# Eight units of attention and experts on one core: per-row values by way of DRAM, and a new order of the steps

## What is computed

```
scores = x @ w + b                        # one score per row
top_scores, top_indices = top_k(scores, k = 204)       # in order of score
h  = x[top_indices] * sigmoid(top_scores)
z  = layernorm(h)
q, k, v = z@Wq.T+bq, z@Wk.T+bk, z@Wv.T+bv
P  = softmax(q k^T / 8)    (rows with q[0]==0 or k[0]==0 are zero)
h  = h + (P v) @ Wo.T + bo
xn = layernorm(layernorm(h)) * gamma + beta
logits = xn @ Wr + br                     # 8 experts
w  = softmax of the two largest logits
h  = h + sum over e of w[e] * (gelu(xn @ W1[e] + b1[e]) @ W2[e] + b2[e])
```

## Time and profile before

| | |
|---|---|
| three runs | 377.15, 377.46, 378.77 us, median 377.46 |
| the profiled execution | 378.94 us, its span 376.8 us |
| mean granted TensorE clock | 0.854 of 2.4 GHz |
| busy: PE, DVE, ACT, POOL | 296.2, 180.7, 148.7, 105.8 us |
| first phase, up to the first `hidden` | 0 to 229.6 us |
| expert steps | 229.6 to 369.4 us |

### The profile page before, as it was taken

The page is one execution under the profiler, slowest core; times in us unless marked ns, Lnnn a source line. Parts: engine busy times, 40 slices in busy tenths (PEclk is TensorE's granted clock), DMA queues, the critical chain, the costliest instruction groups (busy, mean ns, idle before and its releaser), DMA issues.

```text
span 376.8 us, 5432 instructions
## 1 busy us (share of the span) xinstructions
PE 296.2 (79%) x1883; PEld 167.3 (44%) x1883; DVE 180.7 (48%) x541; ACT 148.7 (39%) x328; POOL 105.8 (28%) x97
## 2 busy tenths in 40 slices
PE   1459759598787989888676747979797979797992
PEld 0338546467565666766464442323232323232230
DVE  3764755839458465631316213353544354444331
ACT  1112334333444344353533215444453535354551
POOL 3220200304022030303010110645453544354553
PEclk9975858888696969698886856999998999899997
DMA  2540000000000000000000007808081808170800
GB/s 51 152 121 2 0 0 3 0 3 0 2 0 2 0 3 0 2 0 2 2 0 0 3 20 164 178 5 179 25 191 34 180 12 190 36 168 26 179 22 23
DMA packets 13326, 18.64 MB, mean 49 GB/s; under 512 B 3756, under 2 KB 12276, under 8 KB 12276
## 3 DMA queue, kind: packets, MB, share of 16 engines
q1 hardware_dynamic: 12724, 18.17, 21.5%
q10 hardware_dynamic: 576, 0.13, 0.2%
HBM read 16.42 MB, written 1.88 MB: 49 GB/s over the span
## 4 chain that ended last, share of the span: by engine, by line
PE 61%; DVE 17%; issue 8%; ACT 7%; SPq 3%; POOL 2%; DMA 1%; POOLq 0%; ACTq 0%
PE PD L761 14%; PE PD L771 13%; PE PD L562 5%; DVE pick L843 4%; ACT E L419 4%; PE PD L644 4%; PE PD L614 4%; PE PD L633 3%; DVE nmax L872 3%; PE PD L593 2%; PE PD L550 2%; PE PD L601 2%; PE PD L689 2%; PE PD L661 2%; DVE ye L1026 2%
## 5 line engine op out<-in xcount | busy, mean ns | idle before, releaser
L499 ACT ACTIVATE hid<-PD,b_eff 128x816 f32<-128x816 f32 x64 | 60.1, 940 | 56.0 <-PE PD L761 56.0
L1026 DVE SCALAR_TENSOR_TENSOR ye<-PD,b_col,mb 128x408 f32<-128x408 f32 x64 | 41.0, 642 | 78.6 <-PE PD L771 73.1
L348 POOL TENSOR_TENSOR acc<-acc,ye 128x408 f32<-128x408 f32 x56 | 58.8, 1049 | 60.4 <-DVE ye L1026 59.6
L761 PE MATMUL PD<-uT,w_g 64*128 64x408 f32 x256 | 63.9, 579 | 0.0
L771 PE MATMUL PD<-hid,w_sb 128*64 128x408 f32 x256 | 59.7, 545 | 0.2 <-ACT hid L499 0.2
L327 POOL TENSOR_TENSOR rstd<-veps,neg_half 102x8 f32<-102x8 f32 x8 | 13.1, 1638 | 124.9 <-DVE veps L903 124.9
L419 ACT ACTIVATE E<-PD,nmax 102x204 f32<-102x204 f32 x64 | 26.7, 430 | 35.6 <-DVE nmax L872 35.6
L833 DVE SCALAR_TENSOR_TENSOR ahead<-PD,score,tie 128x256 bf16<-128x256 f32 x64 | 27.1, 479 | 22.4 <-PE PD L550 22.4
L761 PEld LDWEIGHTS PD<-uT,w_g 64*128 64x128 f32 x256 | 20.3, 193 | 31.9 <-issue 29.5
L633 PE MATMUL PD<-ident,E 102*102 102x102 f32 x128 | 18.1, 297 | 19.1 <-ACT rbc L401 13.6
L771 PEld LDWEIGHTS PD<-hid,w_sb 128*64 128x64 f32 x256 | 12.9, 138 | 39.5 <-issue 37.4
(11 more groups left out here) (130 smaller groups left out, 381.5 us busy)
## 6 DMA issues: line engine op xcount, KB each, us to landing
mb<-mixd SPq DMA_DIRECT2D x16, 816.0 KB, 8.0
X<-in_x SPq DMA_DIRECT2D x8, 256.0 KB, 4.9
out<-y SPq DMA_DIRECT2D x8, 204.0 KB
w_raw<-in_L_ffn_W SPq DMA_DIRECT2D x2, 256.0 KB, 3.3
w_sb<-in_L_ffn_W SPq DMA_DIRECT2D x1, 256.0 KB, 3.7
mixd<-mT SPq DMA_DIRECT2D x8, 25.5 KB, 1.5
w_bc<-in_L_tok_w ACTq DMA_DIRECT2D x1, 32.0 KB, 3.8
wq_nat<-in_L_attn_Wq ACTq DMA_DIRECT2D x1, 32.0 KB
```

The source lines that it names most:

```text
L348: pool.tensor_tensor(acc[n % 2][:, :], H[:, n, :] if e == 0 else acc[n % 2][:, :], ye[k % 4][:, :], ALU.add)\
L499: act.activation(hid[k % 2][:, :, :], hid_ps[k % 2][:, :, 0:C], ACT.Gelu, bias=b1_eff[:, e:e + 1]).then_inc(hid_ok, 1)
L761: last = pe.matmul(hid_ps[k % 2][:, p, 0:C], w1_g[halves[p], e, :], uT[halves[p], n, :], start=True, stop=True)
L1026: dve.scalar_tensor_tensor(out=ye[k % 4][:, :], in0=y_ps[k % 2], scalar=b2_col[:, e:e + 1], in1=mb[n % 2][:, e, :], op0=ALU.add, op1=ALU.m ...
```

## The change

1. The score rows, the first inverse deviations, the reciprocals of the softmax sums and the second inverse deviations are no longer spread by PE and copied by ACT. SP writes them to DRAM (`scored`, `rstdd`, `rdend`, `rstd2d`) and reads them back onto all partitions, from one in-order list of 10 DMAs and a load of X per step.
2. `tie` is one table of 257 columns and lies in PSUM, as does `row_no`; `one_hot` is in two halves. `scale_out` on POOL multiplies the attention's output, after a copy of it by ACT (`copy_OT`).
3. `project` is 8 matmuls of 64 x 64 weights and 204 columns in place of two of 128 x 128 and 408 columns, and q and k of the second pair stand on the other half of the partitions.
4. A unit now has lags 0 to 4, and the work of one step is in another order on every engine. The loop has 9 steps.
5. After it comes an end written out by hand, in which the last unit's attention alternates with the first expert steps. PE waits for the first unit alone (`u_ok` = 1). Routing of units 0, 1 and 2 is in steps 7, 8 and the end; that of unit n + 2 within expert steps 0 to 6 of unit n. There are three `mb` tiles.

```diff
-        A_STEPS = UNITS + A_LAG                     # 13
+        A_STEPS = UNITS + 1                         # 9
...
+            def write_scores(u):
+                sp.wait_ge(sc_ok, 2 * u + 2)
+                sp.dma_start(scored[u].rearrange("(b p t) -> p b t", b=UB, t=T),
+                             score[u % 2][:, :].rearrange("p (b t) -> p b t", t=T)).then_inc(scored_ok, 16)
+            def read_scores(u):
+                sp.wait_ge(scored_ok, 16 * (u + 1))
...
+                sp.dma_start(srow[u % 2]..., scored[u].partition_broadcast(P)).then_inc(srow_in[u % 2], 16)
+            def spread(dst, line, done):
+                for i, p in enumerate(halves):
+                    sp.dma_start(dst[p, :].rearrange("p (g q) -> p g q", q=Q),
+                                 line.rearrange("(g p) q -> p g q", p=2)[i].partition_broadcast(D)).then_inc(done, 16)
+            def write_std(u):
+                sp.wait_ge(rstd_ok, u + 1)
+                sp.dma_start(by_row(rstdd[u]), rstd[:, :], allow_slow_non_contiguous=True).then_inc(rstdd_ok, 16)
+            def read_std(u):
+                sp.wait_ge(rstdd_ok, 16 * (u + 1))
...
+                spread(rbc, rstdd[u], rb_in)
...
+            for s in range(A_STEPS):              # SP; unit(...) tests cut
+                load_x(s + 3)
+                write_std2(s - 3); write_den(s - 2); write_std(s); write_scores(s + 2)
+                read_std2(s - 3); read_den(s - 2); read_std(s); read_scores(s + 2)
+                if s >= UNITS - 1:
+                    write_mix(s - (UNITS - 1))
+                    read_mix(s - (UNITS - 1))
...
+            def scale_out(u):                     # POOL
+                pool.wait_ge(OT_ok, u + 1)
+                pool.wait_ge(rd_in, 32 * (u + 1))
...
+                pool.tensor_tensor(attn[:, :], OT[:, :], rdbc[:, :], ALU.mult).then_inc(attn_ok, 1)
...
+            for s in range(A_STEPS):              # ACT; unit(...) tests cut
+                softmax(s - 2, 0); copy_hT(s); squares2(s - 3); squares(s)
+                softmax(s - 2, 1); copy_ET(s - 2, 0); exp_neg(s + 2); copy_ET(s - 2, 1)
+                copy_q(s - 1); copy_k(s - 1); copy_OT(s - 2)
+                if s >= UNITS - 1:
+                    gap_tanh(s - (UNITS - 1))
+                    copy_mT(s - (UNITS - 1))
...
             def project(u):
                 pe.wait_ge(z_ok, u + 1)
                 if u >= 1:
-                    pe.wait_ge(ET_ok, 2 * u - 1)
-                pe.matmul(q_ps, wq_bd[:, :], zT[u % 2][:, :], start=True, stop=True).then_inc(qp_ok, 1)
-                pe.matmul(k_ps, wk_bd[:, :], zT[u % 2][:, :], start=True, stop=True).then_inc(kp_ok, 1)
+                    pe.wait_ge(ET_ok, 2 * u)
+                for i, w in enumerate((wq_bd, wk_bd)):
+                    for pr in range(2):
+                        for p in range(2):
+                            last = pe.matmul(qk_ps[halves[p ^ pr], pr, i * S:(i + 1) * S], w[halves[p], halves[p]],
+                                             zT[u % 2][halves[p], cols(pr, 0, R)], start=True, stop=True)
...
             def centre2(u):
                 pe.wait_ge(h1_ok, u + 1)
                 if u >= 1:
                     pe.wait_ge(u_ok, u)
...
             def hidden(k):
                 n, e = divmod(k, NE)
+                if k == 0:
+                    pe.wait_ge(act_prep, 4)
+                    pe.wait_ge(exp_ok, 2 * UNITS)
+                if k == 1:
+                    pe.wait_ge(ET_ok, 2 * UNITS)
...
+                if k % NE == 0:
+                    pe.wait_ge(u_ok, n + 1)
...
-            pe.wait_ge(u_ok, UNITS)
...
             def compare(u, pr):
-                dve.wait_ge(srow_ok, 2 * u + pr + 1)
+                dve.wait_ge(srow_in[u % 2], 16 * (u // 2 + 1))
...
-                    dve.scalar_tensor_tensor(out=ahead[:, i, :], in0=srow[:, b * N:(b + 1) * N], ...
-                                             in1=tie[:, t, :], ...
+                    dve.scalar_tensor_tensor(out=ahead[:, g, :], in0=srow[u % 2][:, b, :], ...
+                                             in1=tie_ps[:, 1 - t:1 - t + N], ...
...
-                    last = dve.tensor_scalar(pick[:, g, :], row_no[:, :], ...
+                    last = dve.tensor_scalar(pick[:, g, :], row_ps, ...
...
+            for s in range(A_STEPS):              # DVE; unit(...) tests cut
+                residual(s - 3); normalise2(s - 4); normalise(s - 1); row_max(s - 2, 1)
+                var_eps2(s - 3); compare(s + 1, 0); var_eps(s); one_over_den(s - 2); compare(s + 1, 1)
+                copy_v(s - 1); score_sum(s + 2); one_hot(s + 1, 0); gate_value(s + 2); one_hot(s + 1, 1)
+                row_max(s - 1, 0)                 # from step 7 on: route(s - 7, 0..3) among these, part 3 last
...
+            for k in range(8, K):
+                n, e = divmod(k, NE)
+                weighted(k)
+                if n + 2 < UNITS and e in (0, 1, 2, 4):
+                    route(n + 2, (0, 1, 2, 2, 3)[e])
```

More of the change, by code:

```diff
@@ L52, in audio_tower_kernel @@
     G = 4
+    MB = 3
     VX = D + 2
@@ L780, in turn_back @@
                 last.then_inc(backp_ok, 1)
[L782 to L795 removed]
+            pe.wait_ge(pool_prep, 3)
@@ new lines, in _ @@
+            centre2(UNITS - 2)
+            scores(UNITS - 1, 1)
+            logits(2)
+            variance2(UNITS - 2)
+            turn_exp(UNITS - 1, 0)
+            hidden(0)
+            turn_exp(UNITS - 1, 1)
+            attend(UNITS - 1, 0)
+            turn_mix(2)
+            hidden(1)
+            second(0)
+            attend(UNITS - 1, 1)
+            for k in range(2, 5):
+                hidden(k)
+                second(k - 1)
+            centre2(UNITS - 1)
+            hidden(5)
@@ L796, in _ @@
+            second(4)
+            variance2(UNITS - 1)
+            for k in range(6, K):
+                n, e = divmod(k, NE)
+                hidden(k)
+                second(k - 1)
+                if n >= 1 and e == 2:
+                    turn_back(n - 1)
+                if n >= 1 and n + 2 < UNITS:
+                    if e == 0:
                         logits(n + 2)
+                    if e == 6:
+                        turn_mix(n + 2)
+            second(K - 1)
             turn_back(UNITS - 1)
@@ new lines, in _ @@
+                if (u := unit(s, 1)) is not None:
+                    row_max(u, 0)
+                if s == UNITS - 2:
+                    dve.wait_ge(pick_ok, 2 * UNITS)
+                    dve.tensor_copy(fall_s, falling[:, :]).then_inc(dve_prep, 1)
+                    dve.wait_ge(dve_prep, 9)
+                if s >= UNITS - 1:
+                    route(s - (UNITS - 1), 3)
+            residual(UNITS - 2)
+            normalise2(UNITS - 3)
+            row_max(UNITS - 1, 1)
+            for part in range(3):
+                route(2, part)
```

656 lines of the change are left out of this document (326 added, 330 removed).

## The result

The changed kernel takes 463.3 us (median of 4 runs, 461.2 to 463.9) beside 378.0 for the kernel before: a ratio of 1.225, 95% interval 1.220 to 1.230. I had forecast 320, in a range of 302 to 352. The profiled execution has a span of 461.8 us.

| | predicted, us | measured, us |
|---|---|---|
| end of the first `row_max` | 53 | 65.8 |
| from there to `hidden(0)` | 127.2 | 239.9 |
| `hidden(0)` to `hidden(9)` | 25.3 | 33.9 |
| `hidden(9)` to the end of the span | 113.6 | 122.2 |

What follows compares the result with a forecast made beforehand. A ring of hand-overs bounds the first phase, no engine being full; PE bounds the experts. Head 53 + steps 121 + end and ramp 31.5 + experts 103.3 + rest 10.3 = 319.1 us span, forecast 320, range 302 to 352.

Steps and rivals of the forecast that it cites:

- L: Landing of one element-wise line write of 816 4-byte packets: taken as 3.5 us, from bounds of 1.9 to 6.7.
- The DMAs, the unknown: Section on each step's DMAs: issuing ten costs SP 5.5 us; a second ring through them takes 15.5 to 17.5 us.
- rival (a): The DMA ring sets the step, L of 6 to 8: 20.5 us per step, 337 us, up to 350; chance 0.22.
- the ring: Each step's second ring, from `residual` through the 1/den write and reads to `scale_out`: 12 to 14 us + L.
- rival (d): Slower than before: a step's three element-wise writes queue on few engines; 394 us at 28.6 us a step; chance 0.05.
- the first ring: Each step from `row_max` through `score_sum`, `exp_neg`, `copy_ET`, `project` and `scores`: 15.7 to 18.9 us by clock, taken as 18.
- The head: Start to the end of the first `row_max`: 53 us instead of 43, with scores going through DRAM before a comparison.
- The experts: From `hidden(9)` to `hidden(63)`: 103.3 us instead of 120.2, with `mix` made ahead and PE no longer standing still.
- The ramp: From `hidden(0)` to `hidden(9)`: 25.3 us, including 3 us of `turn_back(0)` waiting for `normalise2(7)`.
- the wait of `exp_neg`: On ACT in each step: `exp_neg` waits for `score_sum` ahead of the second `copy_ET`; PE idle some 3 us before `project`.
- the quadrants: `project` on PE as eight matmuls of 204 columns: 0.9 to 1.6 us, with no row to price it.

Runs made afterwards that it cites:

- runs 7, 8 and 10: run 1 plus one unread write of 816 4-byte pieces per unit, neighbours 4, 512 and 64 bytes apart: 387.6, 348.8 and 340.8 us.
- run 7: run 1 plus one write per unit of 816 4-byte pieces, neighbours 4 bytes apart, ahead of the write of 1/den: 387.6 us.
- run 2: The changed kernel with each of the three line writes issued as two DMAs, of 96 and 6 rows: 472.4 us, ratio 1.249.
- run 1: The changed kernel with its three line writes in 102 pieces of 32 bytes, values coming back in another order: 344.2 us, ratio 0.908.
- run 3: The changed kernel with only the write of 1/den in 4-byte pieces, those of 1/std and 1/std2 in 32-byte pieces: 379.4 us.
- run 6: run 5 with SP issuing the write and read of unit 0's scores earlier in its list: 316.0 us, ratio 0.831.
- run 4: The changed kernel with 1/std, 1/den and 1/std2 spread by PE and copied by ACT, without the line DMAs: 335.6 us, ratio 0.887.
- run 5: run 4 with `exp_neg` moved behind `copy_k` on ACT and `gate_value` behind `row_max` on DVE: 322.3 us, ratio 0.849.

## Why the prediction was wrong

**The step that failed is the landing of the element-wise writes, L**, in "The DMAs, the unknown". I took 3.5 us from bounds of 1.9 to 6.7. Measured: 13.2 to 15.0 us in a full step, 7.9 with one such write left, and even the very first, with no other line write near it (issued at 40.01, its read at 46.57), up to 6.6. The upper bound did not hold, and neither row had the pattern: the loads of 4-byte columns read neighbours from DRAM and wrote to separate partitions, the large packets were large. The trace of before had no row of many small pieces written close together into DRAM, and that is what costs (runs 7, 8 and 10). It is also no price per packet: in run 7 the records of these packets are nearly as short as my 7.7 ns, 9 ns, and the landing is late all the same. I had also counted L for one write, though three are issued within 2 us of each other; the sentence "one late write holds all" stood in rival (a), not in the sum.

By the Trainium skill (DMA: Bandwidth & Descriptors, section "Why a DMA increments its semaphore by 16 and not by 1") the write would go to 6 engines. No run here shows to how many it went; run 2 shows that dividing it otherwise does not shorten the landing, so the rule did not decide the time. That the rule gave 15.4 us at 102 ns a packet, beside a measured 15.0, is chance.

**The rule for the ring was right.** "It costs 1 us per step for each us of L over 4.5": L of 15 gives 10.5 us more than 18, a step of 28.5. The measured 34.1 has 5.6 more. Of these 4.0 are the reads (7.1 us from issue to `scale_out` instead of the 3.1 in the ring; in run 1, without the 4-byte pieces, 4.2 to 6.0 in the two steps compared below). The other 1.6 are computing, 12.0 us where I had at most 10.4. It runs at the lower clock (granted 0.50), for which I had allowed; but DVE stands 1.85 us for `variance2` and 0.89 for `variance` in it, and the ring as I listed it has neither.

**What happened is the ring of rival (a) with the queue of rival (d).** `residual` waits for a DMA in every step, the sign of (a), and the writes land after more than 10 us, the sign of (d). (a) stopped at L = 8 and 350 us. (d) had the three writes queue behind each other (run 3) and gave 394 us at a step of 28.6, but by a price per packet on few engines: its own formula, with the mean of 115 ns and 16 engines, gives 17.6 us, not 34. I gave (d) 0.05, since I let the 7.7 ns of a load stand against it.

**The clock came on top.** I had let the clock into the first ring (18 us for 15.7), but priced a longer L at 1 us for each us. In the changed kernel the granted clock is 0.65 in such steps; PE, idle for 13.6 us before 165.29, then takes 1.70 us for `centre2`, against 0.92 in run 6. In run 7 the wait for 1/den is 3.2 us longer than in run 1 (8.1 against 4.9), the step 6 (26.7 against 20.6). Of the rest, 0.3 us are the read's, and 2.6 the computing from `scale_out` to the next write, 12.3 us against 9.7. The two stretches, run 7 and run 1, with the granted clock as the third number from the end:

```profile
134.30:146.50 12.20, 9.88 (x41) 7.42 (x42) 5.33 (x18) 3.52 (x11) 3.39 (x3) 0.50 0.11 37
```

```profile
119.70:129.40 9.70, 7.34 (x47) 5.01 (x44) 4.95 (x18) 4.49 (x16) 3.13 (x3) 0.82 0.18 65
```

**The head was 12.8 us too short.** The scores came 4 us late: the first read was issued at 18.47 and the first comparison started at 25.09, not 21. Since `select` now starts on half of the picks, this cost only 1.6 us there (28.65 instead of 27). The picks read PSUM now, four in 1.68 us, 0.40 apart, not 0.31: 1.4 us for 16 picks. I had carried over the 23.7 us of the old order from the first `select` to the first `scores`; it is 34.1 here (28.65 to 62.70). Order is the larger part of that: `normalise(0)` belongs to the next step, on DVE behind the picks of unit 1 (to 47.0). Then it waits another 6.25 us for the fetched 1/std, so that `zT` starts at 53.27. Run 4, which has the same order and spreads by PE, takes 30.1 (28.11 to 58.20): 4.0 of the 10.4 us are the fetch.

**The experts were right.** They run with no wait for `mix`:

```profile
375.76 0.34 PE L749 MATMUL PD<-ident,mix 102*16 102x102 f32 x2
376.03 0.95 PE L765 MATMUL PD<-uT,w_g 64*128 64x408 f32 x4
376.92 0.91 PE L779 MATMUL PD<-hid,w_sb 128*64 128x408 f32 x4
377.75 0.95 PE L765 MATMUL PD<-uT,w_g 64*128 64x408 f32 x4
```

Against the earlier trace rows the 2.13 us ahead of the transposes are gone and the pair still goes round in 1.72. From `hidden(9)` to `hidden(63)` are 112.0 us, not 103.3: 7.0 of them one stall, `turn_back(0)` waiting for `normalise2(7)`, which I had put at 3 and ahead of `hidden(9)`, and the other 1.7 the low clock behind it (0.57 from 351 to 356). Its cause is again a line write, issued at 338.90 and read from 345.61 on. The ramp's 8.6 us too many have a like cause, the fetched 1/std2 of unit 6 (write 307.90, read from 314.89 on):

```profile
324.20 0.58 DVE L967 TENSOR_TENSOR uT<-PD,rbc 128x408 f32<-128x408 f32 x1 [8.99 <-DMA rbc<-rstd2d]
```

`weighted` stands behind this on DVE, so PE is idle for 5.94 us before the `second` at 325.48. The fetched 1/den of unit 7 (write 308.21, `scale_out` 325.48) adds 0.91 us before `centre2`; around these PE runs partly at the lower clock (0.77 from 305.7 to 340).

**Also right:** the first ring (19.0, 20.5 and 17.0 us in run 4 for my 18), the wait of `exp_neg` and what it costs (run 5), the quadrants at 0.9 to 1.6 us (in the step shown, at the lower clock, 1.64 from 144.98; 0.93 at the full one in run 6).

So the change's parts have opposite signs. The new order, with scores through DRAM and experts begun early, is worth 43 us (378.8 to 335.6 in run 4's comparison), 62 with its two waits mended (run 6). Spreading through DRAM in 4-byte pieces costs 128 over run 4.

## What to carry to other kernels

Before a small tile is transposed by its DMA write, ask where neighbouring pieces land: 816 numbers of 4 bytes into one line of 3.3 KB held up the read of it for 7 to 8 us alone and 13 to 15 us in threes, while the same bytes in rows of 32, or the same pieces 64 bytes apart, hid for the most part behind the list that issued them. Bound a DMA's landing by a row with its own pattern, or say that there is none and keep a bound that can break the forecast, above all where several are issued together and one in-order list waits for each. And when a stall enters a ring that runs through PE, expect it to cost more than itself: here 3.2 us more of waiting made a step 6 us longer, 2.6 of them computing at the lower clock.
